# Scatter destinations from the keys alone, and routing weights computed one turn later

## What is computed

```python
x = x + attention0(layernorm(x))
h = layernorm(x)                                  # 2048 tokens of 256
probs = softmax(h @ gate_w.T)                     # 64 experts
scores, idx = top_k(probs, 8)
pos = arange(P) - starts[e_sorted]                # place of a pair in its expert's queue
valid = pos < C                                   # C = 512 rows for each expert
safe_pos = minimum(pos, C - 1)
xbuf = zeros((E, C, D)).at[e_sorted, pos].set(h[tok_sorted], mode='drop')
y = experts(xbuf)                                 # silu(x Wg) * (x Wu), then Wd
y_pair = y[e_sorted, safe_pos] * (s_sorted * valid)[:, None]
x = x + zeros.at[tok_sorted].add(y_pair)
x = x + attention1(layernorm(x)); x = x + ffn1(layernorm(x))
```

## Time and profile before

| | us |
|---|---|
| median of 3 runs (1454.01 to 1458.57) | 1457.83 |
| the profiled execution, its own time | 1455.02 |
| its span, first to last instruction | 1453.3 |
| PE busy, share of the span | 1287.0, 89% |
| DVE busy | 1000.7, 69% |
| ACT busy | 798.3, 55% |
| POOL busy | 453.0, 31% |

### The profile page before, as it was taken

One profiled execution on the slowest core, in us unless ns is written; L12 is line 12 of the kernel. 1 busy time (PEld: TensorE's weight loads), 2 busy tenths in 40 slices (PEclk: granted clock), 3 DMA queues, 4 the chain that ended last, 5 costly groups with the idle time before them and its releaser, 6 DMA issues.

```text
span 1453.3 us, 28437 instructions
## 1 busy us (share of the span) xinstructions
PE 1287.0 (89%) x9120; PEld 1143.9 (79%) x9120; DVE 1000.7 (69%) x2071; ACT 798.3 (55%) x1543; POOL 453.0 (31%) x490
## 2 busy tenths in 40 slices
PE   4787772199999999759999999999999999999996
PEld 3555552188888888649999999899899998998996
DVE  5576776177777777666767677677676676776655
ACT  4222213066666666536666666666666666666663
POOL 1046767411111111244326225333252162241110
PEclk9998986599999999979999999999999999999998
DMA  8992223378989898741001001000010010110000
GB/s 300 423 361 90 91 88 111 115 256 297 300 293 305 296 300 299 261 133 30 16 16 52 1 27 41 15 29 22 14 47 4 22 43 4 31 30 1 9 1 8
DMA packets 58382, 173.65 MB, mean 119 GB/s; under 512 B 10064, under 2 KB 26960, under 8 KB 56144
## 3 DMA queue, kind: packets, MB, share of 16 engines
q1 hardware_dynamic: 35952, 103.61, 20.2%
q0 software_dynamic: 21504, 67.13, 14.7%
q10 hardware_dynamic: 864, 2.12, 0.4%
HBM read 86.83 MB, written 85.98 MB: 119 GB/s over the span
## 4 chain that ended last, share of the span: by engine, by line
PE 67%; DMA 10%; DVE 9%; issue 6%; ACT 3%; POOL 2%; SPq 1%; another core or an unknown queue 1%; DVEq 0%; ACTq 0%; POOLq 0%
PE bank L787 17%; PE bank L792 9%; DMA experts<-in_moe_in 7%; PE bank L839 6%; PE bank L776 6%; PE bank L822 4%; PE bank L812 4%; PE bank L708 4%; PE bank L880 3%; PE bank L813 2%; PE bank L823 2%; POOL y_rows L426 2%; PE bank L721 2%; PE bank L696 1%; DVE experts L1502 1%
## 5 line engine op out<-in xcount | busy, mean ns | idle before, releaser
L787 PE MATMUL bank<-layer_r 128*128 128x256 f32 x2048 | 310.0, 289 | 10.9 <-issue 4.9
L1293 DVE TENSOR_TENSOR layer_r<-W,layer_r 128x1024 fp32r<-128x1024 f32 (+2 forms) x229 | 256.4, 1121 | 49.8 <-ACT layer_r L1113 49.8
L787 PEld LDWEIGHTS bank<-layer_r 128*128 128x128 f32 x2048 | 268.2, 192 | 15.9 <-issue 12.8
L1113 ACT ACTIVATE layer_r<-W 128x1024 fp32r<-128x1024 f32 (+2 forms) x226 | 221.6, 981 | 59.8 <-PE bank L839 37.3
L525 POOL TENSOR_TENSOR layer<-layer 128x256 f32<-128x256 f32 x120 | 87.3, 728 | 422.2 <-ACT layer L1188 421.7
L708 PE MATMUL bank<-experts_r 128*96 128x512 f32 x768 | 194.3, 402 | 2.8 <-DVE experts_r L1477 2.6
L495 POOL DMA_INDIRECT rows<-y_rows,sidx x128 | 171.0, 1336 | 53.3 <-issue 31.4
L792 PE MATMUL bank<-layer_r 128*128 128x256 f32 x1024 | 176.1, 285 | 0.0
L708 PEld LDWEIGHTS bank<-experts_r 128*96 128x96 f32 x768 | 121.6, 163 | 51.3 <-issue 5.7
L426 POOL DMA_INDIRECT y_rows<-W x128 | 128.6, 1005 | 80.9 <-issue 58.0
L792 PEld LDWEIGHTS bank<-layer_r 128*128 128x128 f32 x1024 | 146.6, 193 | 0.0
(11 more groups left out here) (141 smaller groups left out, 2265.5 us busy)
## 6 DMA issues: line engine op xcount, KB each, us to landing
y_rows<-D SPq DMA_DIRECT2D x32, 1024.0 KB, 39.6
experts<-y_rows POOLq DMA_DIRECT2D x64, 512.0 KB, 4.4
y_rows<-experts SPq DMA_DIRECT2D x64, 512.0 KB, 4.3
W<-in_w SPq DMA_DIRECT2D x32, 416.0 KB, 5.0
experts<-in_moe_in SPq DMA_DIRECT2D x64, 192.0 KB, 4.9
experts<-in_moe_down SPq DMA_DIRECT2D x64, 96.0 KB, 4.4
y_rows<-W POOLq DMA_INDIRECT x128, 2.5
rows<-y_rows,sidx POOLq DMA_INDIRECT x128, 3.2
```

Of the source, the lines that this page charges most:

```text
L787: pe.matmul(out, Whi1[s][:, c * step + at:c * step + at + P], x_[:, c, :], start=(n == 0 and c == 0 and x_ is hi), stop=False, skip_group_ ...
L1113: nc.scalar.activation(Whi1[i % 2][:, 0:W.shape[1]], W, ACT.Copy).then_inc(S["d_whi"], 1)
L1293: return nc.vector.tensor_tensor(dst, src, hi.bitcast(F32), ALU.subtract)
```

## The change

`key` now carries a mark for rows beyond the capacity: the place is bounded by `CAP - 0.75` in place of `CAP - 1`, so such a key ends in a quarter. The destinations are computed from the eight largest keys alone. The row number is rounded into `SLOT`, the difference between the number and its rounding is 0 or a quarter, and four times `DROPPED` times that difference is added, so that the row falls outside the buffer and its scatter does nothing. This is `a_sends`, and it follows `a_places` at once. The rest, which needs the probabilities, is `a_weights`. It runs one turn later, between the first norm of batch `b + 2` and `a_select`, and for the last batch behind the turns. `WGT` is written by the sum itself.

```diff
                 st.done(nc.vector.scalar_tensor_tensor(
-                    out=key, in0=pos, scalar=float(CAP - 1),
+                    out=key, in0=pos, scalar=CAP - 0.75,
...
+            def a_sends(b):
...
+                dve.wait_ge(S["a_pos_steps"], (b + 1) * POS_STEPS)
+                dve.sem_inc(S["dve_carrier"], 1)
+                for t in range(TB):
+                    st.done(nc.vector.max(slotf[:, t, :], key[:, t, :]))
+                st.settled()
+                st.done(nc.vector.tensor_scalar(of_batch(SLOT, b), flat, -1.0, None, ALU.add))
+                st.settled()
+                st.done(nc.vector.scalar_tensor_tensor(out=over, in0=flat, scalar=-1.0, in1=of_batch(SLOT, b),
+                                                       op0=ALU.add, op1=ALU.subtract))
+                st.settled()
+                st.done(nc.vector.scalar_tensor_tensor(out=over, in0=over, scalar=4.0 * DROPPED, in1=flat,
+                                                       op0=ALU.mult, op1=ALU.add))
+                st.settled()
+                st.end()
+                nc.vector.tensor_scalar(scat[b % SENDS], over, -1.0, None, ALU.add).then_inc(S["a_scat"], 1)
+
+            def a_weights(b):
 
                 st = Steps(dve, S["a_slot_steps"], SLOT_STEPS, b)
                 dve.wait_ge(S["a_exp"], b + 1)
                 st.done(nc.vector.reciprocal(rsum, psumx))
-                dve.wait_ge(S["a_pos_steps"], (b + 1) * POS_STEPS)
+                dve.wait_ge(S["a_send_steps"], (b + 1) * SEND_STEPS)
                 st.settled(S["dve_carrier"])
                 for t in range(TB):
-                    st.done(nc.vector.max(slotf[:, t, :], key[:, t, :]))
...
-                st.settled()
                 st.done(nc.vector.tensor_tensor(eq, key.unsqueeze(2).broadcast_to([P, TB, TOPK, E]),
                                                 slotf.unsqueeze(3).broadcast_to([P, TB, TOPK, E]), ALU.is_equal))
...
-                st.done(nc.vector.tensor_reduce(wsum, eq.rearrange("p a b c -> p (a b) c"), AX, ALU.add))
+                st.done(nc.vector.tensor_reduce(of_batch(WGT, b), eq.rearrange("p a b c -> p (a b) c"), AX, ALU.add))
...
                 if b + 2 < NB:
                     a_norm(b + 2)
+                if b > 1:
+                    a_weights(b - 2)
                 if back:
                     a_select(b - 1)
                     a_places(b - 1)
-                    a_slots1(b - 1)
-                    a_slots2(b - 1)
-                    a_slots3(b - 1)
+                    a_sends(b - 1)
...
             for b in range(NB + 1):
                 turn(b, b < NB, b + 1 < NB, b > 0)
+            a_weights(LASTB)
             decay(D1, "decay1_exp", "decay1_ready", range(4))
```

More of the change, by code:

```diff
@@ L226, in build @@
         eq = take([TB, TOPK, E])
-        wsum = take([TB * TOPK])
+        over = take([TB * TOPK])
         scat = [take([TB * TOPK], I32) for _ in range(SENDS)]
@@ L271, in build @@
         a_out_ps a_x1 a_xh2 a_x2T_ps a_x2T a_log_ps a_logit a_ln_steps a_var a_rstd a_ln2_steps a_var2 a_rstd2
-        a_sel_steps a_ntop a_exp a_selb a_rank_ps a_pos_steps a_slot_steps a_scat zeros_ready low_rows_cleared high_rows_cleared
+        a_sel_steps a_ntop a_exp a_selb a_rank_ps a_pos_steps a_send_steps a_slot_steps a_scat zeros_ready low_rows_cleared high_rows_cleared
         b_x_ps b_xhi b_xlo b_whi b_wlo b_dhi b_dlo
@@ L1370, in a_places, with of_batch @@
                 st.end()
-            def a_slots1(b):
+            def of_batch(tensor, b):
+                return tensor[:, b, :] if isinstance(b, int) else \
+                    tensor[:, bass.ds(b, 1), :].rearrange("p a n -> p (a n)")
+            def a_sends(b):
+                flat = slotf.rearrange("p a b -> p (a b)")
+                st = Steps(dve, S["a_send_steps"], SEND_STEPS, b)
+                dve.wait_ge(S["a_pos_steps"], (b + 1) * POS_STEPS)
[14 more added lines that the diff above has]
+            def a_weights(b):
                 st = Steps(dve, S["a_slot_steps"], SLOT_STEPS, b)
@@ L1395, in a_slots2 @@
                 st.settled()
-                st.done(nc.vector.tensor_reduce(wsum, eq.rearrange("p a b c -> p (a b) c"), AX, ALU.add))
+                st.done(nc.vector.tensor_reduce(of_batch(WGT, b), eq.rearrange("p a b c -> p (a b) c"), AX, ALU.add))
                 st.settled()
[L1398 to L1409, removed]
                 st.end()
-            def a_slots3(b):
-                dve.wait_ge(S["a_slot_steps"], (b + 1) * SLOT_STEPS)
-                nc.vector.tensor_copy(scat[b % SENDS], wsum).then_inc(S["a_scat"], 1)
             def turn(b, front, ahead, back):
@@ L1695, in _ @@
             dturn(NB, False, False, True)
-SLOT1_STEPS, SLOT_STEPS = 6, 12
+SEND_STEPS, SLOT_STEPS = 5, 6
 POS_STEPS = 5
```

## The result

| | before | after |
|---|---|---|
| median of 5 runs each, us | 1457.20 (1453.09 to 1458.57) | 1468.40 (1465.19 to 1470.09) |
| ratio, 95% interval | | 1.0097 [1.0072, 1.0122] |
| profiled execution, its own time and span, us | 1455.02, 1453.3 | 1470.09, 1468.4 |

The account below looks back on a forecast made before the run. Each turn was taken as a race of DVE and PE up to L1313, then DVE waiting for PE's logits. 15.6 - 4.2 - 4.7 = +6.7 us, taken as +7: 1462, or 1465 to the median; range 1456 to 1474.

Parts of the forecast that it names:

- the clock falls and stays down: Rival: PE's lower clock in turns 4 to 6 also costs each L1313-to-L1335 stretch about 2 us: 1472; chance 0.13.
- copies held back, turns 3 to 7: Weights delay the logits' copy (L1335) by 4.5 us less DVE's idle time: 15.6 us over turns 3 to 7.
- front halves, turns 4 to 7: End of `a_places` (L1369) to second mask (L1313): shorter by 0.6 us in turn 5, 3.6 in turn 7; -4.2.
- turn 8 and batch 7: End of stage A: scatters come 4.1 us sooner and POOL's last wait shrinks from 0.90 to 0.30: -4.7 us.
- clearing of `y_rows` ended later: POOL's wait for the clearing: its end does not depend on DVE and covers turn 2's 3 us delay; cost 0.
- the shorter path to the next turn: Behind `a_places`: `a_sends` of 1.4 us in place of 5.5, DVE starts the next turn 4.1 us sooner; sum -4.2.
- that case: PE's clock up everywhere: turns 4 and 6 win 1.6 us each, turn 7 about 2.3; sum +1.2 us.
- the prediction's sum by the Trainium skill: Two large two-input weights instructions could hold up batch 7's scatters: sum 2.5 us higher; the prediction took 0.
- POOL is the pace: Rival: the logits' copy does not wait for the weights, POOL's 10.6 us of waits go: 1447; chance 0.09.
- The two balance: Rival: PE's clock stays up and the stall at 254.98 goes, -0.9 us: some 1457 to 1460; chance 0.28.
- What was to show it: Trace: no idle ahead of L1335; L1313 to L1335 some 13 us; POOL's waits longer; last scatter 6 to 8 us later.

Follow-up runs that it names:

- the first look at the kernel before: The kernel before, unchanged, in its first profiled execution: 1455.02 us; 163.4 us from batch 1's first scatter to the first load of the experts' rows (turns' time).
- the second look: The kernel before, unchanged, traced once more: 160.9 us from batch 1's first scatter to the first load of the experts' rows (turns' time).
- The fillers: The changed kernel plus eight PE matmuls whose result nobody reads, ahead of `a_rank` in turns 3 to 7: ratio to before 1.0059 [1.0037, 1.0082].
- no weights: The changed kernel with the weights' products, comparison and sum replaced by one small instruction that writes zeros: ratio to before 0.9956 [0.9933, 0.9978].
- the split kernel: The changed kernel with the weights in two pieces, behind the first mask and behind the second norm: ratio to before 0.9990 [0.9977, 1.0003].
- the weights in the same turn: The changed kernel with the weights put back into the same turn, right behind the new destinations: ratio to before 0.9993 [0.9979, 1.0007].

## Why the prediction came out as it did

The direction, the mechanism and the range were right: slower, because the copy of the logits waits for the weights. The size was about half: +7 us forecast to the median, against 11 us by the medians and 14 by the ratio. The sum's own bounds, 1.2 to 8.3 us and 2.1 more to each side, did not hold it. The stated range did, because its upper end came from the rival of a clock that stays down, which put its loss elsewhere; so far the range held by luck. Term by term, in the two profiled executions:

| term of the sum | forecast us | measured us |
|---|---|---|
| copies held back, turns 3 to 7 | 3.2, 2.85, 2.85, 2.2, 4.5: 15.6 | 2.9, 2.9, 2.9, 2.1, 3.7: 14.6 |
| front halves, turns 4 to 7 | 0, -0.6, 0, -3.6: -4.2 | +1.3, +1.6, +0.3, -0.8: +2.4 |
| `a_rank` itself | 0 | +0.4 |
| turn 8 and batch 7 | -4.7 | -3.9 |
| clearing of `y_rows` ended later | 0 | +2.1 |
| sum to the last scatter (terms are rounded) | +6.7 | +15.7 |

*Copies held back: right.* 4.4 us of weights less the wait that they fill, in each turn; only turn 7 came out 0.8 us smaller than forecast. Turn 3 is taken to the end of its places, as the prediction took it.

*Front halves: the term that was mis-sized, by 6.6 us.* The step that failed is "the shorter path to the next turn" with its clock. The prediction saw that PE would idle some 3 us longer, gave the fallen clock up to 1.6 us in turn 5 as the end of a range, and took about none. The clock was down in turn after turn (0.70 and 0.50 at the start of turn 4, 0.53 to 0.62 at the starts of turns 5 and 6, 0.50 and 0.70 from 216 to 224 us in turn 7). In turn 7 it took back 2.8 of the 3.6 us. The measured +2.4 is against the first look at the kernel before, whose own clock was down in turns 4 and 6; against the second look the term is +4.4. The fillers show it as the cause: with the clock at 1.00, each of the four front halves comes out as the prediction had it for that case. The other part of that case, 2.3 us in the back half of turn 7, no run tested: with the fillers too the clock fell to 0.62 and 0.53 there, and that half took 14.4 us, 4.4 more than before. So the turns' time stayed 4.8 us over the 163.4 of before, where the prediction's lower bound had 1.2. The rival *the clock falls and stays down* had the right part but the wrong place: it put the loss into the back halves, and these are nearly as long with the fillers (12.8 us) as without (13.0).

*The end: right but for a cost taken as none.* Batch 6's first scatter starts 2.2 us behind the places, before 6.4: -4.2, as forecast, and the last wait ahead of batch 7 shrinks by the 0.6. Of that, two scatters of batch 6 that start during the comparison L1407 give back 1.0 and 0.8 us (2.01 and 1.73 us in the rows of POOL above), and the stall beside the L1234 is 0.8 us smaller than the 2.1 of rows 7. The prediction took 0 for this, from the scatter at 154.58 of rows 7 that ran beside an L1385. That row was too little to go by: the scatter started 0.04 us before L1385's start at 154.62, so it was no case of a scatter that starts inside the comparison. Those that do are long, unless they start in its last 0.1 us or so. The same trace has three long ones, at 99.72, 130.94 and 178.66, which the prediction passed over. Here is the last of them, then one in the second look at the kernel before, with the DVE row beside it:

```profile
178.66 1.41 POOL L426 DMA_INDIRECT y_rows<-W  x1 [0.30 <-issue]
```

```profile
175.73 1.41 POOL L426 DMA_INDIRECT y_rows<-W  x1 [0.30 <-issue]
```

```profile
175.07 1.23 DVE L1385 TENSOR_TENSOR W<-W 128x1024 f32<-128x1024 f32 x1
```

The second ends at 177.14, its comparison at 176.30, 0.84 us before. In after, the row at 155.95 above ends at 157.47, 0.84 us behind the L1407 of 155.41 to 156.63, and that at 254.33 again 0.85 us behind it. With no weights, the turns had none of these long scatters. The Trainium skill ("SBUF — State Buffer", "Who interferes with whom") says that a VectorE instruction with two inputs from SBUF contends with a GpSimd instruction that reads SBUF. These rows agree with that, against the prediction's reading. So do two more: in the split kernel a scatter at 88.82 us that started during the product L1416, which also has two, took 1.53 us, and with the weights in the same turn one at 78.16 that started during the sum L1412, which has one, took 0.99 and ended before the sum. No run was made to isolate it. In the middle turns of the changed kernel POOL has waits enough to hide it. In turn 8 it cost 1.8 us, where the prediction's sum by the Trainium skill had 2.5; the scatters held were batch 6's, since those of batch 7 began behind the weights.

*The clearing* ended 2.1 us later in that execution. The prediction took its end as not depending on DVE. Whether the change has a part in it stays open: it differs by 1.4 us between two executions of the kernel before, but was also later in most traces with the new destinations. It is part of the profiled difference of 15.7 us.

*The rivals.* *POOL is the pace* fell twice: its waits grew, and with no weights they remained at 1.78 and 2.92 us. *The two balance* fell with the clock. Its premise, the clock up at the start of turn 5, did hold in the kernel before.

*What was to show it* held for the idle time ahead of L1335, the 13 us back halves, PE as the end of the front halves of turns 4 to 6, POOL's longer waits, and stages B and D. The front halves (9.0 to 10.6 us forecast, up to 11.95 measured) and the last scatter (6 to 8 us later forecast, 15.7 measured) missed, both by the clock term, the second also by the clearing.

Still open: why the clock falls in some executions of the kernel before and not in others, what sets when the clearing ends, and whether the earlier scatters of batch 0 have a part in it.

## What to carry to other kernels

Work that can be put off costs, at its new place, its length less the wait that it fills there: so it goes where its engine waits, in pieces cut to the waits, and not just ahead of an instruction on which the next engine depends, even where the engine as a whole is idle a third of the time. A wait that such a move gives to TensorE can be paid for twice, the second time in the slower work behind it. Read a term from more than one execution before a difference of 1 us is put down to the kernel.

## What the hardware showed

- TensorE's granted clock fell from 1.00 to 0.62 and 0.53 with idle times of 3.6 and 1.3 us close together (turn 5), and the front halves of turns 4 to 6 took 11.0 to 11.95 us. With eight matmuls that nobody needs in the longer of the waits, the clock was 1.00, they took 9.06 or 9.07, and the ratio went from 1.0097 to 1.0059, with intervals that overlap a little.
- The kernel before had the clock at 0.64 in one execution and at 1.00 in another at the same place, with turns' times of 163.4 and 160.9 us.
- An indirect scatter that started during a comparison of 1024 elements a partition with two SBUF inputs (1.22 us) ended 0.84 to 0.87 us after it, in the changed kernel and both looks at the one before, with durations up to 2.0 us. Most others in the turns took 0.97 to 1.19, and one that had started 0.04 us before the comparison took 0.97.
